# A graph network kernel: the edge convolution with features on the partitions

## The reference, cut to what matters

```
h    = x @ W_in                                        # 12500 x 128
W_ij = ssp(f_ij @ Wf1 + bf1) @ Wf2 + bf2               # 200000 x 128, f_ij has 32 columns
W_ij = W_ij * f_ij_cutoff                              # one number per edge
x_ij = h[dst] * W_ij                                   # idx_j is dst
out  = segment_sum(x_ij, src, 12500)                   # idx_i is src
y    = ssp(out @ Wo1 + bo1) @ Wo2 + bo2                # ssp(v) = softplus(v) - log 2
x    = layernorm(x + y)
```

## Time and profile before

| | |
|---|---|
| Median of three runs | 6694.08 us (6691.56 to 6695.51) |
| Profiled execution, its own time | 6709.68 us |
| Its span | 6707.8 us |
| Busy: PE, PEld, DVE, ACT, POOL | 61%, 48%, 50%, 20%, 70% of the span |
| Mean granted TensorE clock | 0.669 of full speed |

### The profile page before, as it was taken

The page is one execution under the profiler, slowest core; times in us unless marked ns, Lnnn a source line. Parts: engine busy times, 40 slices in busy tenths (PEclk is TensorE's granted clock), DMA queues, the critical chain, the costliest instruction groups (busy, mean ns, idle before and its releaser), DMA issues.

```text
span 6707.8 us, 70541 instructions
## 1 busy us (share of the span) xinstructions
PE 4086.0 (61%) x19983; PEld 3205.5 (48%) x19983; DVE 3357.6 (50%) x7053; ACT 1309.4 (20%) x3301; POOL 4716.8 (70%) x4809
## 2 busy tenths in 40 slices
PE   6444444444445543434343455688888879999997
PEld 3333333333333333333333344455555557777796
DVE  7333333333334655555555566533333346777697
ACT  2000000000001100000000000265555545555404
POOL 2777777777775477777777777677777777777604
PEclk9555555555556755555555577787777779999999
DMA  7222222222223422212222233333333347777696
GB/s 276 52 52 53 52 52 52 52 53 52 52 52 108 153 51 51 51 51 51 51 51 51 67 88 88 90 115 106 109 109 107 109 141 220 222 222 222 206 315 199
DMA packets 406899, 714.46 MB, mean 107 GB/s; under 512 B 103872, under 2 KB 180707, under 8 KB 405797
## 3 DMA queue, kind: packets, MB, share of 16 engines
q1 hardware_dynamic: 255622, 387.89, 18.6%
q0 software_dynamic: 150912, 322.24, 17.0%
HBM read 509.82 MB, written 199.90 MB: 106 GB/s over the span
## 4 chain that ended last, share of the span: by engine, by line
POOL 59%; PE 20%; issue 18%; DVE 1%; DMA 1%; ACT 0%; POOLq 0%; SPq 0%; DVEq 0%; ACTq 0%
POOL edge_rows L520 23%; POOL sorted_rows L563 13%; POOL buf_a L520 12%; POOL buf_x L520 11%; PE banks L1507 8%; PE banks L1561 3%; PE banks L1385 3%; PE banks L1496 3%; PE banks L1525 2%; PE banks L1558 1%; PE banks L1387 1%; POOL edge_rows L576 1%; POOL onehot L576 0%; DMA buf_a<-sorted_rows 0%; DVE first_place L780 0%
## 5 line engine op out<-in xcount | busy, mean ns | idle before, releaser
L520 POOL DMA_INDIRECT edge_rows<-messages,idx_stage x1568 | 1528.2, 975 | 686.9 <-issue 477.2
L1411 PE MATMUL banks<-onehot,edge_rows 128*128 128x128 f32 x3136 | 792.5, 432 | 1180.3 <-DMA edge_rows<-messages,idx_stage 1158.8
L1411 PEld LDWEIGHTS banks<-onehot,edge_rows 128*128 128x128 f32 x3136 | 679.9, 320 | 1305.9 <-DMA edge_rows<-messages,idx_stage 1284.3
L563 POOL DMA_INDIRECT sorted_rows<-edge_rows,idx_stage x784 | 777.9, 992 | 273.1 <-issue 231.7
L520 POOL DMA_INDIRECT buf_a<-messages,idx_stage x784 | 777.6, 992 | 238.9 <-issue 238.9
L563 POOL DMA_INDIRECT sorted_rows<-buf_a,idx_stage x784 | 776.4, 990 | 239.1 <-issue 232.7
L520 POOL DMA_INDIRECT buf_x<-messages,idx_stage x784 | 749.8, 956 | 238.9 <-issue 238.9
L939 DVE TENSOR_TENSOR buf_a<-buf_a,banks 128x128 f32 x392 | 113.1, 289 | 1307.7 <-PE banks L1411 1266.8
L1411 PE MATMUL banks<-x_onehot,buf_x 128*128 128x128 f32 x1568 | 406.8, 441 | 585.1 <-DMA buf_x<-messages,idx_stage 585.1
L1411 PE MATMUL banks<-x_onehot,buf_a 128*128 128x128 f32 x1568 | 389.9, 427 | 577.9 <-DMA buf_a<-messages,idx_stage 577.9
L1411 PEld LDWEIGHTS banks<-x_onehot,buf_x 128*128 128x128 f32 x1568 | 349.1, 328 | 642.8 <-DMA buf_x<-messages,idx_stage 642.8
(11 more groups left out here) (164 smaller groups left out, 5561.1 us busy)
## 6 DMA issues: line engine op xcount, KB each, us to landing
buf_a<-sorted_rows SPq DMA_DIRECT2D x593, 288.0 KB, 3.9
messages<-work SPq DMA_DIRECT2D x196, 320.0 KB, 2.2
buf_a<-dst_rows SPq DMA_DIRECT2D x198, 256.0 KB
buf_a<-in_attr SPq DMA_DIRECT2D x198, 128.0 KB
buf_a<-h_in SPq DMA_DIRECT2D x396, 64.0 KB
edge_rows<-messages,idx_stage POOLq DMA_INDIRECT x1568, 2.6
buf_x<-messages,idx_stage POOLq DMA_INDIRECT x784, 2.5
buf_a<-messages,idx_stage POOLq DMA_INDIRECT x784, 2.6
```

Source lines behind the costliest of these rows:

```text
L520: nc.gpsimd.indirect_dma_start(gathered[p][h][:, t, :], None, source, bass.IndirectOffsetOnAxis(ap=idx_stage[:, h, t:t + 1], axis=0),).the ...
L563: nc.gpsimd.indirect_dma_start(sorted_rows, bass.IndirectOffsetOnAxis(ap=idx_stage[:, 2 * u + h, t:t + 1], axis=0), msg_halves[2 * u + h][ ...
L1411: last = nc.tensor.matmul(ps_sums[slot][j], rows_in_slot[:, j * GROUP_TILES + t, :], hot[:, j * GROUP_TILES + t, :], start=(t == 0), stop= ...
```

## The change

Within the convolution the features lie on the partitions until the messages are done. The expansion becomes one matmul of 512 columns per group (the window of h stationary, the one-hot moving), and so does the second filter layer (`Wf2` stationary, `soft` moving). The bias is added by DVE as one number per partition. ACT copies the expansion to `h_edge`, DVE multiplies in place, PE transposes the product tile by tile back into `ps_h`, and ACT copies it with the cutoff as the scale straight into the message slot. On PE `filter_in(k+1)` now stands behind the expansion and the second filter layer, then the transposes, then all four steps of the sums.

```diff
 # ACT, convolution_step
+                    for j in range(2):
+                        act.wait_ge(s_hexp, k * 2 + (j + 1))
+                        act.wait_ge(s_turned, k * 2 + (j + 1))
+                        nc.scalar.activation(h_edge[:, j, :], ps_h[j], ACT.Copy).then_inc(s_hcopy, 1)
                     softplus_half(k + 1)
-                    act.wait_ge(s_hexp, k + 1)
+                    act.wait_ge(s_cut, k + 4)
+                    if r >= 2:
+                        act.wait_ge(s_scat[slot], scattered(r // 2))
                     for j in range(2):
-                        act.wait_ge(s_msg, k * 2 + (j + 1))
-                        act.wait_ge(s_cut, k + 4)
+                        act.wait_ge(s_turned, k * 2 + (j + 1 + SLOT2))
                         for t in range(GROUP_TILES):
-                            tile, i = slice(t * D, (t + 1) * D), j * GROUP_TILES + t
-                            last = nc.scalar.activation(h_edge[:, j, tile], ps_h[j][:, tile], ACT.Copy,
+                            i = j * GROUP_TILES + t
+                            last = nc.scalar.activation(msg_halves[slot][:, i, 0:D], ps_h[j][:, t * D:(t + 1) * D], ACT.Copy,
                                                         scale=cut_stage[:, h, i:i + 1])
-                        last.then_inc(s_hcopy, 1)
+                        last.then_inc(s_msg, 1)
 # DVE, convolution_step: in place of message_group; the one-hots of all four steps now stand at its start
+                    for j in range(2):
+                        dve.wait_ge(s_hcopy, k * 2 + (j + 1))
+                        dve.wait_ge(s_w, k * 2 + (j + 1))
+                        nc.vector.scalar_tensor_tensor(out=h_edge[:, j, :], in0=ps_w[j], scalar=bf2[:, 0:1],
+                                                       in1=h_edge[:, j, :], op0=ALU.add, op1=ALU.mult).then_inc(s_prod, 1)
 # PE, convolution_step
                 for h in range(2):
                     k = r * 2 + h
-                    filter_in(k + 1, 1 - h, (r + h) * 16 + 16)
+                    for j in range(2):
+                        pe.wait_ge(s_win_in[h], r * 32 + 32)
+                        pe.wait_ge(s_spread, k * 2 + (j + 1))
+                        pe.wait_ge(s_msg, k * 2 + (j + 1))
+                        nc.tensor.matmul(ps_h[j], h_win[:, h, j, :], spread[:, h, j * WIDE:(j + 1) * WIDE],
+                                         start=not beyond, stop=True).then_inc(s_hexp, 1)
+                    for j in range(2):
+                        pe.wait_ge(s_soft, k * 2 + (j + 1 + SLOT2))
+                        pe.wait_ge(s_prod, k * 2 + (j + 1))
+                        if adding:
+                            pe.wait_ge(s_added, first + SLOT2)
+                        nc.tensor.matmul(ps_w[j], wf2[:, :], soft_halves[h][:, j, :], start=True, stop=True).then_inc(s_w, 1)
+                    filter_in(k + 1, 1 - h, (r + h) * 16 + 16)
+                    for j in range(2):
+                        pe.wait_ge(s_prod, k * 2 + (j + 1 + SLOT2))
+                        for t in range(GROUP_TILES):
+                            tile = slice(t * P, (t + 1) * P)
+                            last = nc.tensor.transpose(ps_h[j][:, tile], h_edge[:, j, tile], ident[:, :])
+                        last.then_inc(s_turned, 1)
                     if adding:
+                        for i in range(4):
+                            sum_segment(first + i, 4 * h + i, beside_bank[i], first + (1 + SLOT2) if i == 3 else None)
```

More of the change, by code:

```diff
@@ L148, in gnn_program @@
         wf2 = sb("wf2", [P, D])
[L149 to L152, removed]
+        bf2 = sb("bf2", [P, 1])
+        bias = sb("bias", [1, D])
+        bias_rest = sb("bias_rest", [1, 2, D])
+        bias_parts = sb("bias_parts", [1, 3, D], bf16)
+        bias_rows = sb("bias_rows", [3, D], bf16)
         ones_rows = sb("ones_rows", [3, P], bf16)
@@ L1176, in spread_beyond @@
                         dve.wait_ge(s_xagg[2], step + 2)
-                        for t in range(GROUP_TILES):
-                            tile = slice(t * D, (t + 1) * D)
-                            at = h_edge[:, ds(j, 1), tile].rearrange("p o n -> p (o n)")
-                            cut = cut_stage[:, h, ds(j * GROUP_TILES + t, 1)]
-                            last = nc.vector.scalar_tensor_tensor(out=at, in0=ps_w[0][:, tile], scalar=cut, in1=at,
-                                                                  op0=ALU.mult, op1=ALU.add)
-                        last.then_inc(s_xadd, 1)
                     nc.vector.drain()
@@ L1528, in convolution_step @@
                     if adding:
-                        pe.wait_ge(s_msg, k * 2 + SLOT2)
-                        sum_segment(first + 1, 4 * h + 1, beside_bank[1])
-                    if beyond:
-                        with pe.Fori(0, 2) as j:
-                            with pe.Fori(0, BLOCKS) as b:
-                                step = (k * 2 + j) * BLOCKS + b
-                                pe.wait_ge(s_msg, k * 2 + (SLOT2 - 1))
-                                if adding:
-                                    pe.wait_ge(s_added, first + SLOT2)
-                                pe.wait_ge(s_xh_in, step * 16 + 16)
-                                pe.wait_ge(s_xoh[2], step + 1)
-                                pe.wait_ge(s_xadd, step + 1)
-                                for t in range(GROUP_TILES):
-                                    tile = slice(t * P, (t + 1) * P)
-                                    last = nc.tensor.matmul(ps_w[0][:, tile], x_onehot[:, 0, tile], x_h, start=True,
-                                                            stop=True)
-                                last.then_inc(s_xagg[2], 1)
@@ L1549, in convolution_step @@
-                    for j in range(2):
-                        pe.wait_ge(s_soft, k * 2 + (j + 1 + SLOT2))
-                        pe.wait_ge(s_msg, k * 2 + (j - 1 + SLOT2))
-                        if beyond:
-                            pe.wait_ge(s_xadd, (k * 2 + 2) * BLOCKS + 1)
-                        if adding:
-                            pe.wait_ge(s_added, first + (2 * j + SLOT2))
-                        nc.tensor.matmul(ps_w[j], ones_rows[:, :], bias_rows[:, 0, :].unsqueeze(1).broadcast_to([3, 4, D]),
-                                         start=True, stop=False)
-                        for t in range(GROUP_TILES):
-                            last = nc.tensor.matmul(ps_w[j][:, t * D:(t + 1) * D], soft_halves[h][:, j, t * P:(t + 1) * P],
-                                                    wf2[:, :], start=False, stop=(t == GROUP_TILES - 1))
@@ L1563, in convolution_step @@
-                    last.then_inc(s_w, 1)
-                    if adding:
-                        sum_segment(first + 2, 4 * h + 2, beside_bank[2], first + (1 + SLOT2))
-                        pe.wait_ge(s_msg, k * 2 + (1 + SLOT2))
-                        sum_segment(first + 3, 4 * h + 3, beside_bank[3], first + SLOT2)
+                        for i in range(4):
+                            sum_segment(first + i, 4 * h + i, beside_bank[i], first + (1 + SLOT2) if i == 3 else None)
             def convolution(beyond):
```

81 lines of the change are left out of this document (33 added, 48 removed).

## The result

| | before | after |
|---|---|---|
| Median (four runs each) | 6694.74 us (6691.56 to 6695.51) | 6865.24 us (6862.61 to 6869.17) |
| Ratio after / before | | 1.0257, 95% interval 1.0244 to 1.0269 |
| Profiled execution, its span | 6709.68, 6707.8 | 6864.46, 6862.6 |
| First scatter to the one that ends iteration 56 | 1158.0 us, 10.35 per half | 1334.1 us, 11.93 per half |
| From there to the last scatter | 872.8 us, 10.39 per half | 868.5 us, 10.34 per half |

The change makes the kernel 170.5 us slower, where +251 was forecast; the range held it. The two profiled executions differ by 154.8 us: before's was some 15 us above its median, and its first scatter started 13.6 us later than after's. All of the loss lies in the part without sums: +176.1 over its first 112 halves, against -4.3 and -3.3 behind them.

What follows compares the result with a forecast made beforehand. POOL's scatters were taken as the floor, 10.35 us per half; a PE-ACT ring of 12.3 in the first 114 halves (+222) and PE's 10.75 in the last 82 (+29) gave +251, 6945 us, range 6794 to 7110.

Steps and rivals of the forecast that it cites:

- the ring: First 114 halves: new order closes a loop of waits between PE and ACT, 12.3 us per half, some 222 us more.
- Both rivals: Rivals set for the experiments: added work (transposes, ACT's second copies) costs the time, or the matmuls' form does; no chance given.
- The half: First 114 halves: half of PE's work in the ring at the low clock, 0.5 x 4.49 us on top of 10.07.
- The ends of the term: First 114 halves: ring of 10.07 us all at the high clock, 14.56 all at the low.
- Rival A: First 114 halves: clock stays high through the pauses, POOL stays the bound; 6723, or 6694 with cheap transposes; chance 0.14.
- rival B: First 114 halves: clock low all round the ring, 14.56 us, 7203; three quarters low 7073; chance 0.14.
- the last 82 halves: The part with sums: PE sets a period of 10.75 us (10.2 to 11.8), POOL binds below 10.35.
- the +29 us of the term: Last 82 halves: the loss expected from PE's new period of 10.75 us.
- Transposes: Last 82 halves on PE: eight 128x128 float32 transposes at one record each, 1.0 us per half, an estimate without a row.
- rival C: Last 82 halves: transposes cost two records each, 81 x 1.0 us more, 7026; chance 0.13.
- Rival D: POOL's scatters: faster once DVE no longer writes the message slots, 10.2 us per half, 33 us less, 6661; chance 0.04.
- the first part's 222: First 114 halves: the loss expected from the ring, 114 x 1.95 us.

Runs made afterwards that it cites:

- f1_between: Changed kernel with filter_in(k+1) moved between the expansion and the second filter layer on PE; 6701.76 us, ratio 0.9999 to the kernel before.
- e1_between: Changed kernel with filter_in(k+1) between expansion and second filter layer, on another chip; 7864.2 us against 7888.84 before, ratio 0.9972.
- f2_keep: Changed kernel with three useless float32 matmuls of 128x512 in PE's pause, iterations 2 to 56; 6685.73 us, ratio 0.9973 to the kernel before.
- f0_after: The changed kernel as it is, run as a control; 6870.9 us, ratio 1.0250 to the kernel before.
- f3_before_order: Kernel before with only filter_in(k+1) moved behind the second filter layer in the first 57 iterations; 7077.82 us, ratio 1.0560.
- g2_double: Changed kernel with each of the eight transposes of a half issued twice; 7955.21 us, ratio 1.0026 on a chip whose totals are not used.
- g3_keep_turns: Changed kernel with 22 useless transposes of the identity in PE's pause, iterations 2 to 56; 8158.04 us, ratio 1.0273.
- f group: The follow-up runs made on the chip where the kernel before takes 6702.84 us; verdicts in us are taken from it.
- e4_before_order: Kernel before with only filter_in(k+1) behind the second filter layer in the first 57 iterations, on another chip; 8052.43 us, ratio 1.0205.

## Why the prediction was right, and where its size was off

**The mechanism is shown.** Three edits that open or shorten the ring in different places each do what the ring says: the second layer out of it (f1_between: loss gone; e1_between: undisturbed halves 8.12 for 8.16), Ln out of it (9.01 for 9.1), the clock held (f2_keep: 9.82 and POOL bound again). One edit that only closes it on the old kernel makes that slower by 5.6%. Both rivals fall with f1_between, which keeps every added instruction and the form of every matmul and has no loss. What is beside it costs nothing there (doubled transposes, 9.82). The halves of 8.12, 9.01 and 9.82 with doubled transposes come from the chips with gaps; the totals that carry the argument are those of f0_after, f1_between, f2_keep and f3_before_order.

**The clock is shown too.** The forecast took half of the PE work in the ring as low. Measured, it is 2.12 of the 4.49 us that all of it was to cost, 0.47, or 0.41 of the 5.13 that it costs with the expansion counted whole (next paragraph). The half was a choice near the 44% of before, which is (1 - 0.78) / 0.5 from the earlier trace rows, and not worked out from the ring; that it came so close is in part luck. The ends of the term, 10.07 and 14.56, have PE's three blocks at a granted clock of 1.00 and of 0.50. Rival A (the clock stays high) and rival B (it stays low all round) both fall; A is what f2_keep makes by hand, and it ends where A's first part would.

**First mis-sized term, the ring: 12.3 forecast, 11.93 measured, 114 x 0.37 = 42 us.** About 0.25 of it is in the blocks at the high clock, 9.82 for 10.07. In f2_keep, from the copies at 4702.17, the ring is 1.27 to the expansion, 1.96 of expansion, 1.82 of second layer, 2.01 to the second Abs and 2.76 to the next copies. I had 3.28 for the first two terms together, which are 3.23, and 1.91 for the second layer, priced as `filter_in`; and the copies start 0.1 before the end of Ln to which I counted. The other 0.12 is the share of the clock. The sum for the low clock left something out: there the first expansion matmul (half of 3.55, 1.78) outlasts the copies of the second group (1.09), so the whole expansion of 3.55 is on the path and not only its second half. From the copies to the second layer that is 1.27 + 3.55 = 4.82 where I had 4.18, and the ring all at the low clock would be some 15.2 us and not 14.56, an estimate; no run shows such a ring.

**Second mis-sized term, the last 82 halves: 10.75 forecast, 9.94 for PE, 10.34 measured; 81 x 0.41 = 33 us.** The blocks were priced too high: expansion and second layer by 0.30 together (1.71 and 1.81 for 1.91 each), and the sums at 4.03, taken from the earlier trace rows, where they stand in three pieces, against 3.58 in one. The sums were 0.45 too dear, the transposes 0.06. So PE's period went under POOL's floor, the +29 us of the term did not come, and POOL bounds the part, at 10.34. PE has 0.4 us to spare under it; with each transpose doubled (10.82) it would be 0.5 over.

**Transposes, the one cost with no row:** 1.0 us for eight taken, 0.94 measured (0.93 to 0.94 start to start, after); rival C (two records each, 2.0) falls. The 1.0 was my estimate, half of the 2.0 for eight float32 tile matmuls. No run shows transposes as cheap as at the low end of its range, where a period of 10.2 leaves 0.4 us for eight beside the other 9.76; eight more of them in each half cost 0.88 (g2_double). One record (L1534, after) lasts 0.27 us in the median and 0.33 at most, but start to start, which is what PE pays, it is 0.117 us on average, against 0.22 for a float32 matmul of one tile (1.79 for eight): a little over half the price, with one record in place of two. Why a transpose stands as one record is not shown.

**Rival D** (the scatters' floor falls once DVE no longer writes the slots) was right on a size and wrong on the reason. With the ring out of the way the first part takes 10.25 us per half (f1_between, and f2_keep behind its start), and the second 10.26 (f2_keep), where before has 10.35 and 10.39. That is some 22 us of its 33, half in each part. The 0.30 us between scatters is the same; what differs is how long some scatters last. Before, DVE and POOL:

```profile
4901.11 1.28 DVE L1229 TENSOR_TENSOR buf_a<-banks,buf_a 128x512 f32<-128x512 f32 x2
4901.18 0.97 POOL L563 DMA_INDIRECT sorted_rows<-edge_rows,idx_stage  x1 [0.30 <-issue]
...
4902.31 0.87 DVE L1147 TENSOR_SCALAR onehot<-buf_a,part_f 128x512 f32<-128x512 int16 x2
4902.45 1.17 POOL L563 DMA_INDIRECT sorted_rows<-edge_rows,idx_stage  x1 [0.30 <-issue]
```

The scatter beside the writes into the slot (L1229) lasts 0.97 us, the one beside the one-hot of `spread_half` (L1147) 1.17. From 4400 to 5400 all 82 scatters of over 1.00 us overlap L1147, and so do all 57 in f2_keep (L1155 there); the 97 that overlap L1229 and not L1147 last 0.972 at most. A scatter lasts 0.990 us on average in this stretch before and 0.977 in f2_keep, which makes the 0.10 us per half. So the traces put the stretching beside another instruction of DVE than the rival named. No run moved that instruction, so that it is the cause is not shown.

The terms close: the first part's 222 less 42 is 180, measured +176.1 (over 112 halves, since the last two before the sums begin count in the second stretch); the second's 29 less 33 is -4, measured -4.3 with those two halves in it. With -3.3 behind the last scatter that is 168.5, against 170.5 between the medians.

## What to carry to other kernels

Before moving a block on an in-order engine, write down the ring that it closes with the engine that empties its banks, and add it at both clocks: here a ring of 9.8 us lay under the bound of 10.35 and still lost, because its own pause, 3.04 us in the turn shown, was followed by work at a clock of 0.50. Where a stretch of work has a mean clock well under 1 (0.79 here), look first where its pauses stand; moving one call, or three useless matmuls in the pause, was worth all of the 170 us. Costs of a block that is split between others (4.03) are not its cost in one piece (3.58).

## What the runs showed of the hardware that was not expected

- The ring at the changing clock doesn't settle: turns of 12.55 and 11.35 us alternate, with windows of 5.7 and 3.1 us at 0.50 behind the two pauses shown.
- Four sums in a row take 3.58 us, in three pieces 4.03. The breaks between the pieces don't explain it: before, a sum alone took 0.99 to 1.00 and two in a row 2.04. The cause stays open.
- TensorE's granted clock rose from 0.50 to 1.00 under transposes with nothing else on PE, in 12 of the 13 rises from 5000 to 5400 (g3_keep_turns).
- A scatter on POOL lasts 0.97 us in the median, beside DVE's products into the slots too (0.972 at most, before, 4400 to 5400). Beside DVE's one-hot of a half 82 of 100 last over 1.00 us there, and 57 of 158 in f2_keep; 1.17 in the lines of rival D.
- Matmuls of 512 float32 columns in the last 82 halves of after, at a granted clock of 1.00, start 0.86 (expansion), 0.91 (second layer) and 0.96 us (`filter_in`, 33 rows) apart, halves of 1.71, 1.81 and 1.91.
- The same kernel, the one before, takes 6695 us in the first measurement, 6703 on the chip of the f group, and 7889 and 7940 us on the two others. In the traces from these two the instructions last as long (PE's records of L1397 from 900 to 2000 us have a median of 0.421 us in f0_after, e1_between and g3_keep_turns), but many come late: in the first layer of e1_between, PE's records of L1397 at 1000.22 and 1003.02 last 0.37 us each, 2.80 apart, and the profile puts 2.43 us of the wait between them to nothing that it shows. Its chain of waits has 34% under a source that it calls another core or an unknown queue, which the pages of before and after don't have. The halves of e4_before_order's first part come on time all the same. The cause was not found.
